# MLP with per-sequence low-rank adapters: adapters packed per pair of sequences, first-layer adapter factors kept resident, a new order of first loads, and cache-page copies spread differently

## The reference, cut to what matters

```python
# layer 0: gated MLP, F = 1376, with an adapter per sequence
def lora_add(base, inp, A, B):           # Ab = A[id of sequence], Bb = B[id]
    t = einsum('bri,bni->bnr', Ab, inp)
    return base + einsum('bor,bnr->bno', Bb, t) * SCALE
gate = lora_add(x @ W_gate.T, x, A_gate, B_gate)
up   = lora_add(x @ W_up.T,   x, A_up,   B_up)
act  = silu(gate) * up
x += lora_add(act @ W_down.T, act, A_down, B_down)
# layer 1: attention, 32 query heads, 8 key/value heads of 128, RMS norm and rotary tables on q and k,
#          keys and values = 512 cached (16 pages of 32, picked by a block table) + 128 new
# layer 2: x += x @ w_eff.T, w_eff = weight + low-rank delta, snapped to a codebook per group of 128
# layer 3: x += x @ weight[id of sequence].T
```

## Time and profile before

| | |
|---|---|
| median of 3 executions | 1535.65 us (1533.48 to 1535.83) |
| the profiled execution | 1530.62 us, span 1528.9 us |
| mean granted TensorE clock | 0.992 of full speed |
| TensorE busy | 1434.5 us, 94% of the span |
| VectorE, ScalarE, GpSimd busy | 1163.2, 939.4 and 493.7 us |
| HBM read, written | 125.63 MB, 36.72 MB |

### The profile page before, as it was taken

One profiled execution on the slowest core, in us unless ns is written; L12 is line 12 of the kernel. 1 busy time (PEld: TensorE's weight loads), 2 busy tenths in 40 slices (PEclk: granted clock), 3 DMA queues, 4 the chain that ended last, 5 costly groups with the idle time before them and its releaser, 6 DMA issues.

```text
span 1528.9 us, 29324 instructions
## 1 busy us (share of the span) xinstructions
PE 1434.5 (94%) x8014; PEld 1230.2 (80%) x8014; DVE 1163.2 (76%) x2800; ACT 939.4 (61%) x1860; POOL 493.7 (32%) x678
## 2 busy tenths in 40 slices
PE   3998999788999899999999999999999999999988
PEld 2776887667788788888878887888788888888767
DVE  4675767566688788778878886888788778888756
ACT  2333232356677677767767776777677667777643
POOL 4243000155543333333433333343333333433200
PEclk9999999999999999999999999999999999999999
DMA  8678642345321112111111111021112111111214
GB/s 179 207 240 283 197 150 89 98 126 159 111 63 49 50 29 63 60 40 49 50 47 45 57 56 51 29 63 49 51 29 63 60 40 49 50 42 36 97 60 161
DMA packets 104275, 131.03 MB, mean 86 GB/s; under 512 B 11861, under 2 KB 79590, under 8 KB 98838
## 3 DMA queue, kind: packets, MB, share of 16 engines
q1 hardware_dynamic: 98678, 109.49, 23.6%
q0 software_dynamic: 5024, 17.93, 3.9%
q10 hardware_dynamic: 384, 1.41, 0.7%
HBM read 125.63 MB, written 36.72 MB: 106 GB/s over the span
## 4 chain that ended last, share of the span: by engine, by line
PE 75%; issue 9%; DVE 7%; ACT 2%; POOL 2%; DMA 2%; POOLq 1%; SPq 1%; ACTq 0%; DVEq 0%
PE proj_ps L1170 16%; PE sc L1210 12%; PE o_ps L1247 12%; PE proj_ps L1268 11%; PE ring L1229 8%; PE proj_ps L1026 4%; PE o_ps L1026 4%; PE sc L1026 3%; PE ring L1283 2%; PE ring L1295 1%; PE ring L1026 1%; DMA wd_raw<-in_WdT 1%; POOLq L584 1%; DVE w_l L1426 1%; POOL v_pages L585 1%
## 5 line engine op out<-in xcount | busy, mean ns | idle before, releaser
L1699 DVE TENSOR_TENSOR pTl<-ring,pTh 128x512 fp32r<-128x512 f32 x320 | 215.1, 689 | 72.8 <-ACT pTh L851 69.3
L833 ACT ACTIVATE p_sb<-p_sb,bias,rstd 128x640 f32<-128x640 f32 x256 | 235.8, 921 | 46.7 <-DVE bias L1675 46.7
L637 POOL TENSOR_TENSOR rstd<-var,half_neg 128x4 f32<-128x4 f32 x64 | 80.6, 1259 | 532.1 <-DVE var L1736 483.5
L851 ACT ACTIVATE pTh<-ring 128x512 fp32r<-128x512 f32 x320 | 184.4, 599 | 55.2 <-PE ring L1229 54.4
L1665 DVE CUSTOM_DVE_ANT_0 p_sb<-sc,mask 128x640 f32<-128x640 f32 x256 | 209.1, 817 | 4.4 <-PE sc L1210 0.8
L1229 PE MATMUL ring<-ident,p_sb 128*128 128x128 f32 x1280 | 183.5, 274 | 5.7 <-DVE p_sb L1691 3.4
L1170 PE MATMUL proj_ps<-wh,xh 128*128 128x512 f32 (+1 forms) x512 | 179.7, 351 | 8.9 <-issue 8.2
L1229 PEld LDWEIGHTS ring<-ident,p_sb 128*128 128x128 f32 x1280 | 153.9, 141 | 33.5 <-DVE p_sb L1691 3.7
L1170 PE MATMUL proj_ps<-wl,xh 128*128 128x512 f32 (+1 forms) x512 | 172.6, 337 | 0.0
L1170 PE MATMUL proj_ps<-wh,xl 128*128 128x512 f32 (+1 forms) x512 | 172.2, 336 | 0.0
L1210 PE MATMUL sc<-kTh,qTh 128*128 128x320 f32 x512 | 163.5, 319 | 1.8 <-DVE kTl L1800 1.8
(11 more groups left out here) (247 smaller groups left out, 3632.7 us busy)
## 6 DMA issues: line engine op xcount, KB each, us to landing
k_pages<-in_k_cache SPq DMA_DIRECT2D x128, 128.0 KB, 3.4
v_pages<-in_v_cache POOLq DMA_DIRECT2D x128, 128.0 KB, 3.5
k_raw<-k_pages SPq DMA_DIRECT2D x64, 256.0 KB, 3.1
v_raw<-v_pages SPq DMA_DIRECT2D x64, 256.0 KB, 3.0
stage<-in_Wqkv SPq DMA_DIRECT2D x32, 384.0 KB, 3.5
w_raw<-in_WguT SPq DMA_DIRECT2D x20, 512.0 KB, 5.7
stage<-in_WoT SPq DMA_DIRECT2D x32, 256.0 KB, 3.3
w_raw<-in_W3T SPq DMA_DIRECT2D x8, 1024.0 KB, 5.4
```

What stands on the lines that cost most here:

```text
L833: act_e.activation(p_sb[:, p_slot(u, h), :], p_sb[:, p_slot(u, h), :], ACT.Exp, bias=bias[:, h:h + 1], scale=rstd[:, u.k % 2, h:h + 1], ac ...
L851: act_e.activation(pTh[:, c, :], ring[c % 2][:, :], ACT.Copy).then_inc(S["pth"], 1)
L1699: v.tensor_tensor(pTl[:, c, :], ring[c % 2][:, :], pTh[:, c, :].bitcast(F32), ALU.subtract).then_inc(S["ptl"], 1)
```

## The change

- **Adapters per pair.** Of the 128 adapter rows only the 32 (`PAIR`) of two sequences are used for the 256 columns of these two. `lora_in` and `lora_down` become two sets of matmuls over 256 columns. `lora_out` and the adapter's part of `down` stack high, low and high parts in 96 rows (`STACK`), so that one pass makes all three products: 2 matmuls over 256 columns in place of 3 over 512, and 4 in place of 12 in `down(hf, FC)`. The stacked factors `wb` are made by ScalarE with 4 copies of 32 x 256 per chunk in the first half and 6 in the second, and by VectorE with 2 subtractions, in place of one instruction of 128 x 256 on each. `mask_t` and `low_t` work on 32 rows; ScalarE's `high_t` copies twice. Memsets of tails go.
- **A resident.** The A factors are loaded once (into the buffer of the W_down blocks), split into `la_h` and `la_l`, and used by both halves; a half has 11 W blocks.
- **First loads.** SyncE first loads x chunk by chunk and the first W block in two pieces; ScalarE's queue issues the small index loads; the other adapters' loads move to GpSimd's queue, four sequences before the first use and four later. TensorE starts with `gate_base(0)` and `up_base(0)`, and only then `lora_in`.
- **Order.** Angles, `reduce_angles` and `sines` move from the start into chunks 1 to 3; masks, tables, codebook and `weight2` move one or two chunks later; `weight2(1, 0)` moves from chunk 10 to the joint of the halves. ScalarE and VectorE take the next W block ahead of the adapter's; the low half of W is still VectorE's.
- **Pages.** 4 keys per W block from block 4 on (72 before attention), 8 in each of 7 units; 5 values per chunk for 20 chunks (100 before attention), and 4 in each of the first 7 units, now between `k_sin` and `k_pow`.

```diff
-         8: ((3, 0), (3, 1)), 9: ((3, 2), (3, 3)), 10: ((3, 4),)}
+PARTS = {5: ((0, 0),), 6: ((0, 1),), 7: ((0, 2),), 8: ((0, 3),), 9: ((0, 4),),
+         12: ((1, 1), (1, 2)), 13: ((1, 3), (1, 4)), 15: ((2, 0), (2, 1)), 16: ((2, 2), (2, 3)), 17: ((2, 4),),
+         19: ((3, 0), (3, 1)), 20: ((3, 2), (3, 3)), 21: ((3, 4),)}
 LEAD = 12
-EARLY = 5
+SP_PAGES = 72
+POOL_PAGES = 100
 LORA2 = 64
...
+la_h = l0_sb("la_h", [P, 2, C, B * RANK], F32R)
+la_l = l0_sb("la_l", [P, 2, C, B * RANK], F32R)
+lb = l0_sb("lb", [P, 2, F])
+wb = l0_sb("wb", [P, 2, 2, 2, P], F32R)
...
+def wait_w(engine, q):
+    engine.wait_ge(S["w_hi"], q + 2)
+    engine.wait_ge(S["w_lo"], q + 2)
...
-load_w(0)
-load_w(1)
+load_x_chunk(0, 0)
+load(w_raw[:, 0, 0:C * P], ins["WguT"][0, :, 0:C * P], w_first[0])
+load_x_chunk(0, 1)
+load_x_chunk(0, 2)
+load_x_chunk(0, 3)
+load(w_raw[:, 0, C * P:], ins["WguT"][0, :, C * P:], w_first[1])
+sp.wait_ge(S["idx_in"], 48)
+for b in range(B):
+    load(wd_raw[:, 0:2, :].rearrange("p a n -> p (a n)")[:, b * 2 * C * RANK:(b + 1) * 2 * C * RANK],
+         ins["AguT"][bass.ds(adapter(b), 1), :, :].rearrange("a p n -> (a p) n"), S["la_in"])
+    if b == 3:
+        load_w(1)
 load_w(2)
+sp.wait_ge(S["xl_set"], C)
+for c in range(C):
+    load_x_chunk(1, c)
 load_w(3)
-sp.wait_ge(S["xl_set"], C)
...
+for q in range(4, 2 * FC):
     load_w(q)
-    if q == 5:
+    if q == 7:
         load_group(0)
     if 8 <= q < 11:
         load_wd(q - 8)
-    copy_keys(3)
-    if q == CH - 1:
+    if q == 12:
+        load_wd(3)
         store_group(0)
         load_group(1)
-load_w(CH)
-load_w(CH + 1)
-load_wd(3)
-copy_keys(6)
-sp.wait_ge(S["xl_set"], 2 * C)
-load(x_sb[:, HALF:, :], ins["x"][HALF:].rearrange("b t n -> t b n"), x_in[1])
-for q in range(CH + 2, 2 * CH):
-    load_w(q)
-    n = q - CH + 2
-    load_wd(n if n < FC else n - FC + CH)
-    copy_keys(5)
-    if q == CH + 5:
+    if q == 14:
+        sp.wait_ge(S["xl_set"], 2 * C)
+        load(x_sb[:, HALF:, :], ins["x"][HALF:].rearrange("b t n -> t b n"), x_in[1])
+    if 14 <= q < 21:
+        load_wd(q - 10)
+    if q == 16:
         store_group(1)
         load_group(2)
-    if q == CH + 9:
+    if q == 20:
         store_group(2)
         load_group(3)
+    copy_keys(4)
+for n in range(3):
+    load_wd(CH + n)
...
+if u.turn is None and u.k < B - 1:
     copy_keys(8)
...
+def load_adapters(hf):
+    for b in range(hf * HALF, (hf + 1) * HALF):
+        n = B * NPP + b
+        a = pool.value_load(idx[0:1, n:n + 1], min_val=0, max_val=15)
+        pool.dma_start(lb[b * RANK:(b + 1) * RANK, :, :],
+                       ins["BguT"][bass.ds(a, 1), :, :, :].rearrange("a r k f -> (a r) k f")).then_inc(adapter_in[hf], 16)
+        pool.dma_start(lad[:, b, 0:FC - 1, :],
+                       ins["AdT"][bass.ds(a, 1), :, :, :].rearrange("a p c r -> (a p) c r")).then_inc(adapter_in[hf], 16)
+        pool.dma_start(lad[0:FTAIL, b, FC - 1, :],
+                       ins["AdTt"][bass.ds(a, 1), :, :].rearrange("a p r -> (a p) r")).then_inc(adapter_in[hf], 16)
+load_adapters(0)
...
-    pool.wait_ge(S["gate_up"], 2 * n + 1)
-    copy_values(8 * (n - 2), 8 * (n - 1))
+    valued[0] += many
+for n in range(2, 2 * FC):
+    pool.wait_ge(S["w_hi"], n + 2)
+    copy_values(5)
...
+if u.turn is None and u.k < B - 1:
+    copy_values(4)
...
+def high_w(q):
+    w = P if q % FC < FC - 1 else FTAIL
+    act_e.wait_ge(w_in[q % 2], 16 * ((q + 1) // 2))
+    if q >= 2:
+        act_e.wait_ge(S["gate_up"], 2 * (q - 1))
+    act_e.activation(w_h[:, q % 2, :, :, 0:w], w_blocks(q % 2)[:, :, :, 0:w], ACT.Copy).then_inc(S["w_hi"], 1)
...
+def high_wb(n):
+    hf, m = divmod(n, FC)
+    w = rows(m)
     if m == 0:
-        if hf:
-            act_e.wait_ge(S["gate_up"], 2 * hf * FC)
-    elif m == 1:
-        act_e.wait_ge(S["t_done"], 2 * hf + 2)
-    else:
-        act_e.wait_ge(S["gate_up"], 2 * (hf * FC + m - 1))
-    if q == 1:
-        act_e.wait_ge(S["lb_in"], B * 16)
-    act_e.activation(w_h[:, q % 2, :, 0:C, :], w_blocks(q % 2), ACT.Copy)
-    act_e.activation(w_h[:, q % 2, :, C, :], lb[:, :, m * P:(m + 1) * P], ACT.Copy).then_inc(S["w_hi"], 1)
+        act_e.wait_ge(adapter_in[hf], 3 * HALF * 16)
+    if n >= 2:
+        act_e.wait_ge(S["gate_up"], 2 * (n - 1))
+    for j in range(2):
+        q = 2 * hf + j
+        src = lb[q * PAIR:(q + 1) * PAIR, :, m * P:m * P + w]
+        for r in (0, 1) if hf == 0 else (0, 1, q):
+            i = act_e.activation(wb[r * PAIR:(r + 1) * PAIR, n % 2, j, :, 0:w], src, ACT.Copy)
+    i.then_inc(S["wb_hi"], 1)
...
+        act_e.wait_ge(S["wd_used"], before * FC + k + 1)
+if n < FC:
+    r = rows(n)
+    act_e.activation(wd_h[0:r, q % 2, :], wd_source(q)[0:r, :], ACT.Copy).then_inc(S["wd_hi"], 1)
+    return
+for j, dst in enumerate((wd_h, wd_l)):
+    own_rows = 2 * hf + j
+    src = lbd[own_rows * PAIR:(own_rows + 1) * PAIR, :]
+    for r in (0, 1) if hf == 0 else (0, 1, own_rows):
+        i = act_e.activation(dst[r * PAIR:(r + 1) * PAIR, q % 2, :], src, ACT.Copy)
+i.then_inc(S["wd_hi"], 1)
...
+high_x(0, 0)
+high_first_w(0)
+high_x(0, 1)
+high_x(0, 2)
+high_x(0, 3)
+high_first_w(1)
+high_la(0)
+high_la(1)
+high_wb(0)
 high_t(0, 0)
+high_w(1)
 high_t(0, 1)
-sines()
-split_w(2)
+high_wb(1)
 silu(0)
 for n in range(1, FC):
+    high_w(n + 1)
+    if n == FC - 1:
+        copy_delta(1)
     high_act(n - 1)
-    if n == 4 or n == FC - 1:
-        copy_delta(n // 9)
-    split_w(n + 2)
+    high_wb(n + 1)
+    if n == 3:
+        sines()
+    if n == 5:
+        copy_delta(0)
     if n >= FC - 3:
         split_wd(n - (FC - 3))
     silu(n)
 high_x(1, 1)
 high_x(1, 2)
...
+        a_h, a_l = la_h[:, k, c, ranks], la_l[:, k, c, ranks]
+        for n, (a, x) in enumerate(((a_h, xT_h), (a_h, xT_l), (a_l, xT_h))):
+            i = mm(bank[0:PAIR, ts], a, x[:, c, ts], start=c == 0 and j == 0 and n == 0, stop=c == C - 1 and j == 1 and n == 2)
 i.then_inc(S["t_done"], 1)
...
 def lora_out(n, k):
     hf, m = divmod(n, FC)
-    q = hf * CH + m + 1
...
+    pe.wait_ge(S["t_hi"], 2 * (3 * hf + k + 1))
+for j in range(2):
+    ts = slice(j * 2 * T, (j + 1) * 2 * T)
+    i = mm((gate_ps, up_ps)[k][0:w, ts], wb[0:STACK, n % 2, j, k, 0:w], tb[:, k, ts], start=False, stop=j == 1)
+i.then_inc(S["gate_up"], 1)
...
+        i.then_inc(S["wd_used"], 1)
+else:
+    mm(seq_ps[j], tb[:, 2, ts], (wd_h, wd_l)[j // 2][0:STACK, q % 2, :], start=False, stop=True
+       ).then_inc(S["down"], 1)
...
+def low_w(q):
+    w = P if q % FC < FC - 1 else FTAIL
+    dve.wait_ge(S["w_hi"], q + 2)
+    v.tensor_tensor(w_l[:, q % 2, :, :, 0:w], w_blocks(q % 2)[:, :, :, 0:w],
+                    w_h[:, q % 2, :, :, 0:w].bitcast(F32), ALU.subtract).then_inc(S["w_lo"], 1)
...
+def low_wb(n):
+    hf, m = divmod(n, FC)
+    w = rows(m)
+    dve.wait_ge(S["wb_hi"], n + 1)
+    for j in range(2):
+        q = 2 * hf + j
+        mine = slice(q * PAIR, (q + 1) * PAIR)
+        i = v.tensor_tensor(wb[2 * PAIR:3 * PAIR, n % 2, j, :, 0:w], lb[mine, :, m * P:m * P + w],
+                            wb[mine, n % 2, j, :, 0:w].bitcast(F32), ALU.subtract)
+    i.then_inc(S["wb_lo"], 1)
...
-split_w(2)
+low_x(0, 0)
+low_first_w(0)
+low_x(0, 1)
+low_x(0, 2)
+low_x(0, 3)
+low_first_w(1)
+dve.wait_ge(S["own_set"], 3)
+low_la(0)
+low_la(1)
+low_wb(0)
+dve.wait_ge(S["scale_exp"], 1)
+v.reciprocal(scales[:, 1, :], scales[:, 0, :]).then_inc(S["scale_inv"], 1)
+dve.wait_ge(S["iota_set"], 2)
+v.tensor_copy(key, key_i).then_inc(S["key_copied"], 1)
+mask_t(0, 0)
+low_t(0, 0)
+low_w(1)
+mask_t(0, 1)
+low_t(0, 1)
+low_wb(1)
 gated(0)
 for n in range(1, FC):
     low_act(n - 1)
-    split_w(n + 2)
+    low_w(n + 1)
+    low_wb(n + 1)
     if n >= FC - 3:
         split_wd(n - (FC - 3))
     if n == 1:
+        angles()
+        reduce_angles(0)
+    elif n == 2:
+        reduce_angles(1)
+    elif n == 3:
         masks()
-    elif n == 2:
+    elif n == 4:
         rotary_tables()
-    elif n == 3:
         codebook()
-    elif n < 9:
-        weight2(0, n - 4)
-    elif n == FC - 1:
-        weight2(1, 0)
+    for part in PARTS.get(n, ()):
+        weight2(*part)
```

More of the change, by code:

```diff
@@ L32 @@
 HT = HALF * T
-FP = FC * P
 CH = FC + 1
+STACK = 96
+PAIR = 2 * RANK
 D, HQ, HK = 128, 32, 8
@@ L285, in cond_resid_kernel @@
         w_in = [sem(f"w_in_{n}") for n in range(2)]
+        w_first = [sem(f"w_first_{k}") for k in range(2)]
+        xT_in = [sem(f"xT_in_{c}") for c in range(C)]
+        adapter_in = [sem(f"adapter_in_{n}") for n in range(2)]
         wd_in = [sem(f"wd_in_{n}") for n in range(3)]
@@ new lines, in lora_in, with base @@
+                i.then_inc(S["t_done"], 1)
+            def base(n, k):
+                m = n % FC
+                w = rows(m)
+                bank = (gate_ps, up_ps)[k]
+                for c in range(C):
+                    if n == 0 and k == 0:
+                        pe.wait_ge(S["xh_set"], c + 1)
+                        pe.wait_ge(S["xl_set"], c + 1)
```

(37 more changed lines are left out.)

332 lines of the change are left out of this document (137 added, 195 removed).

## The result

The changed kernel took 1549.86 us (median, 1548.05 to 1550.77) beside 1534.57 us for the kernel before: a ratio of 1.0099, interval 1.0081 to 1.0116. It is 15 us slower; 1501 was predicted, and even the range (1490 to 1514) missed it. The profiled execution took 1549.1 us, its span is 1547.5.

A forecast was written before the change was run, and what follows sets the result against it. TensorE, busy 94%, was taken as the bound, except in the first half, where VectorE's waits rule. Gains 5.7 + 5 + 2 + 10.9 + 11 = 34.6 took 1530.6 to 1496.0, median 1501; own range 1494 to 1508, wider 1490 to 1514.

The forecast's parts named there:

- After that nothing of the change reaches.: Everything behind the first eight attention units: the change was to have no effect there, so no gain or loss.
- the slower one (DMA engines, 1540): MLP chunks: rival that DMA engines set their pace, up to 45 us more over 20 chunks, 1540; chance 0.04.
- Second half, -10.9: Chunks 12 to 21: TensorE is the bound and packing saves 10.9 us, new length 90.6; bounds 6 to 11.
- The term for TensorE: Second half: 45 matmuls per chunk become 41, 0.91 x 10, and `down(0,11)` saves 1.8; sum 10.9 us.
- the third rival: Second half: packing brings nothing because VectorE and its waits set the pace; -10.9 becomes -1, 1511; chance 0.07.
- First half, -5: `gated(0)` to `gated(10)`: VectorE's chain shortens from 85.4 to 80.3 us, gain 5; bounds +9 and -3.
- taken as 0.6 per chunk: First half: VectorE's usual wait before L1424, which the change removes because ScalarE takes W first.
- the upper bound that was taken: First half: VectorE's subtraction on 32 rows priced at the full 0.425 us, not a quarter, 0.11.
- Start, -5.7: Start to `gated(0)`: 36 us instead of 41.71, gain 5.7; bounds 31 and 44.
- Joint, -2: Between the halves: `down(0,0)` covers the wait for `lad_l`; 20.7 us instead of 22.8, gain 2.
- Early units, -11: First eight attention units: 133.6 us, gain 11, with four value copies before `k_pow` mostly hidden.
- the first rival: Early units: copies run at full pitch before `k_pow`, four cost 4.6 us, 10.8 together, about 1512; chance 0.13.

The follow-up runs named there:

- two increments: Changed kernel with two semaphore increments more on ScalarE ahead of the loop: 1524.05 us, ratio 0.9933 to the kernel before.
- 51: Kernel before with 51 semaphore increments more at ScalarE's start, none of the change: 1550.07 us, ratio 1.0094.
- without the side work: Changed kernel, 16 semaphore increments, value copies late, `weight2` parts 1 to 3 left out for groups 1 to 3 (output not the reference's): 1499.89 us.
- the better order of the experiments: Changed kernel, 16 semaphore increments, late value copies, ScalarE's `wb` copies behind silu, VectorE's low part of `wb` right behind `gated`: 1510.0 us.
- 16 increments: Changed kernel with 16 semaphore increments more at ScalarE's start, nothing else: 1524.0 us, ratio 0.9912 to the kernel before.
- the move out of this place: Changed kernel with 16 semaphore increments, an early unit's four value copies moved to the end of GpSimd's step: 1519.27 us, ratio 0.9877.
- the last two runs: Changed kernel, 16 increments, late copies, `wb` work behind silu and `gated`: 1510.0 us; same with six value copies per chunk, two or none per early unit: 1507.53.
- the three kernels with the second stand: Changed kernel (1549.86 us), changed kernel with one semaphore increment more on ScalarE (1548.62), kernel before with 51 more (1550.07).

## Why the prediction was wrong, point by point

The forecast for the profiled execution was 1496.0 us, it took 1549.1. Of these 53 us the later units are 18, the second half 16, the early units 9, the first half 5, and the rest 5.

- **"After that nothing of the change reaches."** This step failed, and it alone is worth the whole loss: +18.2 us in units 8 to 63, at six returns, of 18.5 between the two traces. No instruction of the loop was changed, but ScalarE's program ahead of it grew, and the entry came to the last two instructions of a fetched piece, so that each return stands for two pieces in a row and the clock falls behind it. Shown from both sides: two increments take the loss out, 51 bring it into the kernel before. None of the rivals had it; the slower one (DMA engines, 1540) is refuted, since with six value copies per chunk the two halves took no longer (81.0 and 100.4 us). The view that would have warned is the idle time with no releaser at the returns before: 3.11 us, and 4 us longer units.
- **Second half, -10.9.** The term for TensorE was right: 103.4 less 10.9 is 92.5, and 92.1 was measured without the side work. VectorE's work was right too: 77.3 before and 7.2 more is 84.5, measured 83.9. Wrong was its waiting, put at 7 us (0.7 per chunk for `act_h`, measured 7.3): it was 24.2. It lacked the wait for `wb`, 7.7 us, since six copies and not four are made there (the 0.4 per copy itself was right: 2.55 for six), and waits of 4.6 for W_down's parts. And it was an average: a chunk with two parts of `weight2` takes 12.3 to 13.9 us, one without is over early and waits for TensorE, ScalarE or W_down, and this time is not carried over. The mechanism was that of the third rival (packing brings nothing, 0.07), but that put the stretch at -1, and it came to +4.8.
- **First half, -5.** Gain 0. VectorE's work grew as forecast, by 12.6 us (57.8 to 70.4 busy; the prediction's terms give 12.7). Its waits fell by 12.3 (27.5 to 15.2 idle in the stretch) and not by 17.3. The two long ones went, but the usual wait for `wb` or its forerunner, taken as 0.6 per chunk, had been 4.5 in all and left 0.8, and not forecast were 3.2 for `wd_h` and 1.1 for `silu`. The subtraction on 32 rows costs 0.417 us, so the upper bound that was taken was right: rows don't count here. The Trainium skill (VectorE: DVE Perf Modes, The TRN2 errata), which gives the formula that the prediction cites for an fp32 add, comes to 0.424 us; this subtraction agrees within 2%. With the better order of the experiments the half takes 81.9 us, near the forecast of 80.3.
- **Start, -5.7.** 37.6 against 36: the mechanism held, and the terms as written add up to 36 to 38. First matmul at 9.0, so x and the first piece of W did come ahead of the adapters, for which ScalarE waited until 23.2. TensorE waits for the A factors, to 22.3 us after and to 26.7 with 16 increments, and `gated(0)` moves with them, 36.4 to 41.3 in the traces of the changed kernel and its variants; what moves the A factors was not tried.
- **Joint, -2.** -0.6: TensorE's idle ahead of `lora_down(10)` fell from 5.24 to 3.71 us and no further. The 12 matmuls that were to cover it had ended at 121.8, 1.4 us before `gated(10)` began at 123.2, and the clock was at 0.50 from 126.5 to 129.9. (The prediction's terms for this stretch add up to 20.3 and not 20.7.)
- **Early units, -11.** -2.0. The queue doesn't run ahead in units 0 and 1: the first rival (full pitch, 0.13) was right in them, at its price of 4.6 us for `k_pow`. TensorE waited 8.6 us for `scale_k` there, and the two units took 35.7 us, where 29.2 was forecast and the kernel before took 28.7. Units 2 to 7 took 17.6 to 18.2, forecast 17.3 to 17.4; the move out of this place gave back 5.4 of eight units in the traces. What makes the rest 0.4 us or more longer than a later unit are the copies: with four of them, late, units 3 to 6 take 17.8 to 18.2, with two or none 17.2 to 17.3 (the last two runs).

What stays open: why the kernel before, whose entry stood elsewhere, also fetched two packets but stood 3.1 and not 2.2 us (that the first of them, 0.56 us behind the branch, was of what follows the loop and delayed the other is a guess); how long a fetched piece is in instructions; where the 0.6 us ahead of unit 0 and the 1.5 behind unit 63 come from; and why the load of W_down is 6.6 us late in one chunk.

## What to carry to other kernels

A change far away can move the entry of a hot loop: compare first the units that nothing touched, and if each return of a loop costs more, put a few idle instructions ahead of the loop in the program of the engine that stands still, and measure again; only then judge the change, against the old kernel shifted alike. Cheapening the bound engine pays only up to the next engine's worst chunk: add up its work and its waits chunk by chunk, with side work where it lies, and follow the order on the engine that feeds it. A copy issue that looks half price behind long work has its full pitch where the queue can't run ahead.

## What the runs showed of the hardware

- One instruction more or less ahead of a loop changed the whole kernel by 24.6 us (1548.62 to 1524.05): at the first return ScalarE stood 2.1 us for one 8 KB packet of its program, or 5.05 us for two in a row (over six returns 2.1 to 2.7, and 4.7 to 5.1).
- Idle times of TensorE of 3.31 to 4.18 us ahead of `output` were followed by the 1.2 GHz level (clock 0.50) at all 18 returns of the three kernels with the second stand. At the 66 returns of the other kernels, idle 1.03 to 2.33 us, the clock fell right behind the idle at one (2.12 us, at 935 in the kernel before) and within 8 us at seven more. At 291.7 us after it fell behind 2.24 us.
- VectorE's subtraction of 256 elements per row took 0.417 us on 32 rows and 0.426 on 128; GpSimd's took 0.72 to 1.17, 0.82 in the mean, for the same 32 rows.
